# A graph kernel whose start-up norms go by quarters for six tiles instead of four

## The reference

```
mask = adj > 0
head = mask / max(sqrt(sum(mask * mask, rows)), 1e-12)
inc  = adj + head
y    = x + (inc @ x) / sum(inc, rows)
out  = (y - mean(y)) / sqrt(var(y) + 1e-5)        # over the 256 columns
```

## Time and profile before

| | us |
|---|---|
| median of 3 runs | 427.29 (424.83 to 427.61) |
| the profiled execution, its own time | 428.19 |
| its span, first to last instruction | 426.4 |
| PE busy | 396.4 |
| DVE busy | 370.9 |
| POOL busy | 344.2 |
| ACT busy | 343.3 |

### The profile page before, as it was taken

How to read it: one execution, slowest core, us unless ns; L and a number is a source line. 1 busy time by engine, 2 the same in 40 slices (tenths; PEclk the granted TensorE clock), 3 DMA queues, 4 the chain that set the end, 5 groups by cost and what they waited for, 6 DMA issues and landing times.

```text
span 426.4 us, 8925 instructions
## 1 busy us (share of the span) xinstructions
PE 396.4 (93%) x2174; PEld 349.5 (82%) x2174; DVE 370.9 (87%) x750; ACT 343.3 (81%) x450; POOL 344.2 (81%) x273
## 2 busy tenths in 40 slices
PE   1299987989999999999999999999999999999995
PEld 0277866868888888888888888888888888888884
DVE  0986776899999999999999999999999999999942
ACT  4874968989998888888989889898988988886300
POOL 3110386799999999999999999999999999999960
PEclk9999998999999999999999999999999999999999
DMA  8999986666766666666666666776666676670010
GB/s 231 258 233 244 261 220 182 173 190 200 215 188 197 194 203 216 213 196 192 200 184 200 186 200 202 221 212 190 200 186 199 186 199 194 206 221 25 26 38 12
DMA packets 38220, 79.86 MB, mean 187 GB/s; under 512 B 9536, under 2 KB 21824, under 8 KB 38208
## 3 DMA queue, kind: packets, MB, share of 16 engines
q1 hardware_dynamic: 37824, 78.68, 64.8%
q10 hardware_dynamic: 384, 1.05, 0.9%
HBM read 75.50 MB, written 4.19 MB: 187 GB/s over the span
## 4 chain that ended last, share of the span: by engine, by line
PE 70%; issue 3%; POOL 2%; DVE 2%; ACT 0%; POOLq 0%; DVEq 0%
PE edge L699 35%; PE edge L708 18%; PE edge L655 15%; POOL inc_split L380 2%; DVE inc L465 1%; PE sums L650 1%; DVE incT L481 1%; POOL inc_split L385 0%; ACT scaled L237 0%; POOLq L45 0%; POOL rstd L364 0%; DVE rows L533 0%; DVE rows L508 0%; DVE rows L512 0%; DVE stats L516 0%
## 5 line engine op out<-in xcount | busy, mean ns | idle before, releaser
L380 POOL TENSOR_TENSOR inc_split<-incT,inc_split 128x832 fp32r<-128x832 f32 x120 | 236.9, 1985 | 8.9 <-DVE incT L481 6.1
L699 PE MATMUL edge<-x_split,inc_split 128*128 128x512 f32 (+1 forms) x810 | 195.4, 392 | 0.0
L226 ACT ACTIVATE sign_out<-raw,sign_bias 128x1024 bf16<-128x1024 f32 x128 | 146.3, 1143 | 32.0 <-DMA raw<-in_adj_dram 30.5
L699 PEld LDWEIGHTS edge<-x_split,inc_split 128*128 128x128 f32 x810 | 145.9, 188 | 26.7
L465 DVE SCALAR_TENSOR_TENSOR inc<-raw,scaled 128x1024 f32<-128x1024 f32 x128 | 153.5, 1199 | 4.1 <-ACT scaled L237 4.1
L481 DVE STREAM_TRANSPOSE incT<-inc 128x1024 f32<-128x1024 f32 x128 | 155.8, 1227 | 0.2
L237 ACT ACTIVATE scaled<-raw,norm 128x1024 f32<-128x1024 f32 x128 | 141.7, 1107 | 13.2 <-POOL norm L390 6.6
L708 PEld LDWEIGHTS edge<-x_split,inc_split 128*128 128x128 f32 x780 | 99.1, 194 | 2.3
L708 PE MATMUL edge<-x_split,inc_split 128*128 128x256 f32 x780 | 100.0, 286 | 0.0
L655 PE MATMUL edge<-x_native,incT 128*128 128x256 f32 x384 | 92.2, 389 | 1.1 <-DVE count L447 0.7
L655 PEld LDWEIGHTS edge<-x_native,incT 128*128 128x128 f32 x384 | 71.9, 194 | 10.1 <-DVE incT L481 0.8
(11 more groups left out here) (35 smaller groups left out, 119.5 us busy)
## 6 DMA issues: line engine op xcount, KB each, us to landing
raw<-in_adj_dram SPq DMA_DIRECT2D x504, 128.0 KB, 2.6
rows<-in_x_dram SPq DMA_DIRECT2D x32, 128.0 KB, 2.1
out_dram<-rows SPq DMA_DIRECT2D x32, 128.0 KB, 1.7
x_stage<-in_x_dram SPq DMA_DIRECT2D x8, 224.0 KB, 10.3
x_stage<-in_x_dram SPq DMA_DIRECT2D x8, 192.0 KB, 9.8
raw<-in_adj_dram ACTq DMA_DIRECT2D x8, 128.0 KB, 5.4
x_native<-in_x_dram SPq DMA_DIRECT2D x4, 192.0 KB, 7.3
```

Of the source, the lines that this page charges most:

```text
L226: nc.scalar.activation(sign_out[:, :], raw[:, s, q, :], ACT.Sign, scale=SIGN_SCALE, bias=sign_bias[:, 0:1], accum_out=part_sums[:, s, 1, q ...
L380: nc.gpsimd.tensor_tensor(lo_of(s, q), incT[:, s, 0:SPLIT, q, :], hi_of(s, q).bitcast(fp32), ALU.subtract).then_inc(lo_by_pool, 1)
L699: last = nc.tensor.matmul(edge[s][:, c0:c1], inc_split[s][:, 0, b, :, :].rearrange("p q j -> p (q j)"), x_split[:, b, :, :].rearrange("p h ...
```

## The change

- `EARLY` goes from 4 to 6, and tiles 2 and 3 get their degree sum by a product of its own (`sum_degree`) instead of the joint one. PE, DVE, ACT and POOL each get a written list for the tiles up to 5; the lists of the last tiles are written out too, in the order that they had.
- x is loaded so that a run in memory holds two rows (2 KB, before 1 KB). To match, the transpose reads `inc` with a step of two elements: chunk 2b+l holds the columns 64b+2j+l. `X_AT` goes from 0, 7, 14, 20 to 0, 6, 14, 20.
- `sign_out` becomes int8 in two slots, so that a sign waits for the one before the last. Its bias is given as a constant, not as a tile.
- y is built in place; `y_main` goes, and `y_first` waits for the normalisation of tile t-2.
- SP loads the residual of tile 1 behind the adj rows of tile 2, and stores tile t-5 behind tile t's loads (before t-4).
- In the loop the joint sum goes from hi chunk 3 to hi chunk 6.

```diff
-        sign_out = sb("sign_out", [P, COLS], bf16)
+        sign_out = sb("sign_out", [P, 2, COLS], mybir.dt.int8)
...
-    x_v = x.rearrange("(g b j) d -> g j b d", g=G, j=SQ)
+    x_v = x.rearrange("(g b j l) d -> g j b (l d)", g=G, j=SQ, l=2)
...
-        X_AT = [0, 7, 14, 20, SPLIT]
+        X_AT = [0, 6, 14, 20, SPLIT]
-        EARLY = 4
+        EARLY = 6
...
 SP:
+            load_x(0)
+            load_x(1)
+            load_x(2)
+            load_x(3)
+            load_residual(0, 0, False)
+            for k in range(G):
+                load_quarter(2, 0, k, True)
+            load_residual(1, 1, False)
+            for k in range(G):
+                load_quarter(3, 1, k, True)
+            for t in range(4, 6):
+                for k in range(G):
+                    load_quarter(t, t % 2, k, True)
+                if t == 5:
+                    store(0, 0)
+                load_residual(t - 2, t % 2, True)
...
-                    store(t - 4, s)
+                    store(t - 5, 1 - s)
...
 ACT:
-                    act.wait_ge(signs_ready, G * t + q)
+                    act.wait_ge(signs_ready, G * t + q - 1)
...
             sign_early(0, 0)
             sign_early(0, 1)
             scale_early(0, 0)
+            scale_early(0, 1)
             sign_early(0, 2)
-            scale_early(0, 1)
             sign_early(0, 3)
+            sign_early(1, 0)
             scale_early(0, 2)
+            sign_early(1, 1)
             scale_early(0, 3)
-            sign_early(1, 0)
-            sign_early(1, 1)
+            sign_early(1, 2)
...
 DVE:
-                nc.vector.transpose(incT[:, s, :, q, :],
-                                    inc[:, q, :].rearrange("p (b j) -> p b j", j=SQ)).then_inc(incT_ready, 1)
+                nc.vector.transpose(incT[:, s, :, q, :].rearrange("p (b l) j -> p b l j", l=2),
+                                    inc[:, q, :].rearrange("p (b j l) -> p b l j", j=SQ, l=2)).then_inc(incT_ready, 1)
...
+                dve.wait_ge(result_ready, t - 1)
+                after(t, 2)
+                step(nc.vector.scalar_tensor_tensor(y[:, s, :], edge[s][:, D:2 * D], rdeg[:, :], xres[:, s, :],
+                                                    ALU.mult, ALU.add))
...
             count_early(0, 0)
+            inc_quarter(0, 0, 0, reuse=False, reuse_deg=False)
             count_early(0, 1)
-            inc_quarter(0, 0, 0, False, False)
+            transpose_quarter(0, 0, 0, slot_split=False, reuse_slot=False)
             count_early(0, 2)
...
+            inc_quarter(0, 0, 2, reuse=False, reuse_deg=False)
+            inc_quarter(0, 0, 3, reuse=False, reuse_deg=False)
             count_early(1, 0)
             count_early(1, 1)
             count_early(1, 2)
+            transpose_quarter(0, 0, 2, slot_split=False, reuse_slot=False)
+            transpose_quarter(0, 0, 3, slot_split=False, reuse_slot=False)
...
 PE:
-            native_tile(0, 0, {1: lambda: sum_early(1, 2), 6: lambda: sum_early(1, 3)}).then_inc(edge_ready, 1)
-            native_tile(1, 1, {2: lambda: sum_degree(0, 0), 5: lambda: sum_early(2, 0), 9: lambda: sum_early(2, 1),
-                               15: lambda: sum_early(2, 2), 22: lambda: sum_early(2, 3),
-                               28: lambda: sum_early(3, 0)}).then_inc(edge_ready, 1)
-            tile(2, 0, {("native", 0): lambda: sum_degree(1, 1), ("native", 1): lambda: sum_early(3, 1),
-                        ("native", 4): lambda: sum_early(3, 2), ("hi", 6): lambda: sum_early(3, 3),
-                        ("lo", 8): lambda: sum_quadrants(2, 0, early=True)}, first=True)
-            tile(3, 1, {("hi", 18): lambda: sum_quadrants(3, 1, early=True)})
+            sum_early(1, 2)
+            unsplit_chunks(0, 0, 0, B, {4: lambda: sum_early(1, 3), 18: lambda: sum_degree(0, 0)})
+            unsplit_chunks(1, 1, 0, B, {3: lambda: sum_early(2, 0), 8: lambda: sum_early(2, 1),
+                                        14: lambda: sum_early(2, 2), 17: lambda: sum_early(2, 3),
+                                        22: lambda: sum_degree(1, 1), 25: lambda: sum_early(3, 0),
+                                        31: lambda: sum_early(3, 1)})
+            tile(2, 0, {("native", 1): lambda: sum_early(3, 2), ("hi", 11): lambda: sum_early(3, 3),
+                        ("hi", 18): lambda: sum_early(4, 0), ("lo", 1): lambda: sum_degree(2, 0)}, first=True)
+            tile(3, 1, {("native", 0): lambda: sum_early(4, 1), ("native", 4): lambda: sum_early(4, 2),
+                        ("hi", 6): lambda: sum_early(4, 3), ("hi", 14): lambda: sum_early(5, 0),
+                        ("lo", 7): lambda: sum_degree(3, 1)})
+            tile(4, 0, {("native", 0): lambda: sum_early(5, 1), ("native", 2): lambda: sum_early(5, 2),
+                        ("hi", 3): lambda: sum_early(5, 3), ("hi", 14): lambda: sum_quadrants(4, 0, early=True)})
+            tile(5, 1, {("hi", 9): lambda: sum_quadrants(5, 1, early=True)})
+            SUMS_AT = ("hi", 6)
```

More of the change, by code:

```diff
@@ L427, in _ @@
+            norm_early(4, 3)
             low_quarter(3, 1, 3)
-            with pool.Fori(2, PAIRS - 1) as u:
-                tile(2 * u, 0)
-                tile(2 * u + 1, 1)
-            tile(TILES - 2, 0)
-            tile(TILES - 1, 1, more=False)
-            for s in range(2):
-                rstd_of(TILES - 2 + s, s)
+            low_quarter(4, 0, 0)
+            norm_early(5, 0)
+            rstd_of(2, 0)
+            round_quarter(4, 0, 1)
+            round_quarter(4, 0, 2)
+            norm_early(5, 1)
@@ L611, in _ @@
-            tile(TILES - 2, 0, PAIRS - 1)
-            tile(TILES - 1, 1, PAIRS - 1, more=False)
-            normalise(TILES - 3, 1, PAIRS - 2, True)
-            for s in range(2):
-                for _ in residual(TILES - 2 + s, s, PAIRS - 1):
-                    pass
-                normalise(TILES - 2 + s, s, PAIRS - 1, True)
+            transpose_quarter(1, 1, 0, slot_split=False, reuse_slot=False)
+            inc_quarter(1, 1, 2, reuse_deg=False)
+            inc_quarter(1, 1, 3, reuse_deg=False)
@@ new lines, in _ @@
+            count_early(4, 3)
+            inc_quarter(4, 0, 2)
+            y_second(2, 0)
+            statistics(2, 0)
+            count_early(5, 0)
+            transpose_quarter(4, 0, 2)
+            inc_quarter(4, 0, 3)
+            mean_variance(2, 0)
+            variance_eps(2, 0)
+            transpose_quarter(4, 0, 3)
+            degree(3, 1)
+            inverse_degree(3, 1)
+            normalise(2, 0, 1)
+            count_early(5, 1)
+            inc_quarter(5, 1, 0)
+            y_first(3, 1, 1)
@@ new lines, in _ @@
+            variance_eps(26, 0)
+            transpose_quarter(28, 0, 3)
+            inc_quarter(29, 1, 0)
+            degree(27, 1)
+            normalise(26, 0, 13)
+            inc_quarter(29, 1, 1)
+            inverse_degree(27, 1)
+            transpose_quarter(29, 1, 0)
+            y_first(27, 1, 13)
+            inc_quarter(29, 1, 2)
+            y_second(27, 1)
+            count_of(30, 0)
+            transpose_quarter(29, 1, 1)
+            statistics(27, 1)
+            inc_quarter(29, 1, 3)
@@ new lines, in _ @@
+            transpose_quarter(31, 1, 1)
+            statistics(29, 1)
+            inc_quarter(31, 1, 3)
+            mean_variance(29, 1)
+            transpose_quarter(31, 1, 2)
+            variance_eps(29, 1)
+            transpose_quarter(31, 1, 3)
+            degree(30, 0)
+            normalise(29, 1, 14)
+            inverse_degree(30, 0)
+            y_first(30, 0, 15)
+            y_second(30, 0)
+            statistics(30, 0)
+            mean_variance(30, 0)
+            variance_eps(30, 0)
@@ L619, in _ @@
+            degree(31, 1)
+            normalise(30, 0, 15)
+            inverse_degree(31, 1)
+            y_first(31, 1, 15)
+            y_second(31, 1)
+            statistics(31, 1)
+            mean_variance(31, 1)
+            variance_eps(31, 1)
+            normalise(31, 1, 15)
         @block.tensor
```

613 lines of the change are left out of this document (410 added, 203 removed).

## The result

The changed kernel takes 422.51 us (422.11 to 423.53, 7 runs); beside it the kernel before took 427.61. The ratio is 0.9883 with a 95% interval of 0.9849 to 0.9917, so 5.1 us or 1.2% less. The forecast was 8.5 us. The profiled execution took 423.53 (before 428.19). Now and then an execution takes over 1.5% longer than the fastest of the same kernel; such executions are left out of all comparisons here.

The account below looks back on a forecast made before the run. PE was taken as the bound, idle only in start-up. Tile 4 ending at 92.0 instead of 100.72 was to gain 8.5 us, later tiles and tail unchanged: 427.29 - 8.5 = 418.8; forecast 416.5 to 421.5 (64%), range 415.5 to 423.5.

Parts of the forecast that it names:

- the walk: Start-up worked out in order from single durations: tile 0 begins at 25.2, tile 1 ends 54.7, tile 4 ends 92.0 us.
- rival A: Start-up: one new PE wait of 2 to 2.5 us with half clock behind it; gain 4 to 4.5, 423.0 us; 18%.
- When PE can start tile 0: Start-up: with the new engine orders PE begins tile 0 at 25.2 us instead of 21.13.
- Six native chunks take 2.59 us, 0.432 each, so 64 chunks take 27.7: Tiles 0 and 1 on PE: their 64 chunks priced at 0.432 us each, 27.7 us in all.
- Tiles 2 to 4: Start-up on PE: waits of 2.52 and 1.31 us go; three tiles take 37.3 us, ending at 92.0.
- the ten extra sums: Tiles 2 to 4: ten more small sums in PE's list, 0.17 us each, 1.7 in all.
- The nine sums of tiles 0 and 1: Tiles 0 and 1: nine small sums on PE, taken at 0.2 us each, 1.8 in all.
- The 2.52 us go, and with them the clock's fall, 1.7: Tile 2: PE's wait before the joint sum goes, 2.52 us, and the work lost to the lower clock, 1.7.
- x sooner by 1.2 us: Loading x in 2 KB runs: 251 GB/s instead of 234, so x ends 1.2 us sooner.
- The full tiles: The loop after start-up: 27 tiles keep their period of 11.87 us.
- The strided transpose: DVE transposes reading every second element: taken at 1.23 us each, the same as contiguous ones.
- rival C: DVE: the strided read slows transposes; 434 us at 1.5 us each, 533 at the far bound; 6%.

Follow-up runs that it names:

- the dummies: Changed kernel with six unused fp32 products of 256 columns on PE between tile 1's sums, ahead of tile 0: 420.88 us, ratio 0.9831; second run 420.96, 0.9860.
- the added wait: Changed kernel with a PE wait for tile 3's last transpose at lo chunk 2 of tile 2: 426.52 us, ratio 0.9971; without it 422.00, 0.9877.

## Why the prediction was right, and where its size was off

**Right in the walk, lucky in the range.** The waits went where the prediction said, but the gain is 5.1 and not 8.5. The time is inside the stated range only because that range had been widened for rival A, a new wait of 2 to 2.5 us with the clock at half behind it (423.0). No such wait came. The time came near that rival's figure for another reason, the slow first chunks, which stand in no rival. That is luck.

**When PE can start tile 0: right.** 25.2 worked out, 24.82 measured. Of the 0.4, about half is quarter (1,0)'s data, there at 16.34 in place of 16.58; the rest fits signs that take 0.1 less.

**"Six native chunks take 2.59 us, 0.432 each, so 64 chunks take 27.7": this step failed**, by 2.9 us, and it is most of what is missing. The price was taken from a full tile, where PE is busy without a gap. Behind 17 us in which PE did nothing but small sums with gaps, it runs the first chunks at half pace. The trace of the kernel before shows it, too, in a line that I passed over as part of the stretch in which PE waits for x:

```profile
22.45 4.52 PE L655 MATMUL edge<-x_native,incT 128*128 128x256 f32 x10
26.80 0.28 PE L629 MATMUL sums<-part_sums,quad_sum 128*128 128x1 f32 x2
```

Ten records, five chunks, take 4.35 us up to the next sum, 0.87 each, though x_native and incT were there: the first of them ran at 21.13. It cost nothing that shows there, since PE still had to wait for the last piece of x at 37.19. The change moved PE's start behind the point where x covers it, and so uncovered the slow stretch. The granted clock in the records does not tell: the window of PE from 24 to 31 us of the changed kernel (busy, count, clock, DMA share, GB/s) says 1.00, while each chunk takes twice its time. That is the pace of the 1.2 GHz level; that the clock was at that level is inferred from the pace.

```profile
24.00:31.00 7.00, 6.18 (x16) 1.00 1.07 237
```

The Trainium skill, page "TensorE: Matmul & The Clock Gate", section "Part 1: The HAM clock gate", gives the lower rate as the idle state and warns that the trace's clock events have been seen to be unreliable. Both fit this case: 0.9 us a chunk behind the quiet stretch, and 1.00 in the clock column beside it. The prediction looked at clock only where the records showed a fall.

**Tiles 2 to 4: all waits gone, right.** 37.3 us worked out, 37.95 measured. Three times 11.868 is 35.6. If the rest is all the ten extra sums, they cost 2.35, 0.235 each and not 0.17. That is 0.65. The nine sums of tiles 0 and 1 come to 0.23 each, worked out in the same way.

**The reason for the 8.5 was half right.** "The 2.52 us go, and with them the clock's fall, 1.7" treats the two as PE's loss. Taken away alone they gave 0.5 us by the medians (0.8 by the ratio, its interval reaching from 0 to 1.6). Other engines set the pace of that stretch: PE then waited for POOL's round, and with that moved, at the next joint sum. That the joint norm of tile 4 holds them is the likeliest reading, argued and not shown by itself. The prediction's list of waits also left out 0.88 us ahead of the sum of (3,3) at 62.19 and 0.35 us ahead of tile 4. Its walk came out near the truth all the same, because it priced the new lists from end to end and not the waits removed. In the changed kernel the sentence would be true: there a wait costs its length, and by the mean clocks the fall as well in about half of the runs.

**x sooner by 1.2 us: not shown, and without effect.** 240 GB/s, not 251, in the range of what 1 KB runs reach (234 and 245). With tile 0 slow at its start, x had cover in any case; with the dummies ahead it has almost none, and there the run's length was not tested. My reading of 234 against 261 as the price of short runs doesn't hold. The Trainium skill, page "DMA: Bandwidth & Descriptors", section "Specifications", by which 512 B is enough, fits what the runs show here: no gain from 1 KB to 2 KB.

**The full tiles: 11.887 in place of 11.868**, 0.5 us in 27 tiles, not foreseen. With the joint sum at hi 3 again the even period is 11.873, but the first loop tile loses it there. The rest is open.

**The strided transpose: right**, 1225 ns against 1226; rival C falls. The Trainium skill, page "SBUF — State Buffer", section "Door 1: The DMA port swizzle", has two halves here; the trace agrees with the one by which two accesses per 16-byte line go at full rate.

Together: 8.5 - 2.9 (slow chunks) + 0.4 (start) - 0.25 (sums in tiles 0 and 1) - 0.65 - 0.5 (full tiles) = 4.6, and the profiled executions differ by 4.66. The 0.2 allowed for a wait in tile 5 did not come; it is about what separates the two readings of tile 5's start before, 100.72 and 100.56.

Rival A's prices were right in size (a wait of 2.3 costs 2.6, and 1.3 more in about half of the runs), but no such wait came.

## What to carry to other kernels

Price the first products behind a quiet stretch at half pace, whatever the granted clock says: look for a chunk that takes twice its usual time, and ask what covers it. Then fill the quiet stretch with products nobody needs, if the engine has nothing else to do; here six of them are worth about 2 us. Where a forecast's number comes true by a path that none of its theories names, count it as a miss. And before a wait is counted as a gain, look at who sets the pace: in a stretch that others set, a removed wait only moves to the next sum.

## What the hardware showed that was not expected

- The half-speed stretch lasts for four chunks in some traces of the changed kernel and its variants (the changed kernel beside the added wait, the sum at hi 3) and six in others (its first trace, and the one beside the dummies), 3.6 to 5.7 us. By these figures it spreads the time by up to 1 us.
- In the traces, waits of 2.52 us and 2.45 us were followed by a fall of the granted clock (0.57 from 71 to 75 us, 0.65 from 78 to 82 us), one of 2.32 us was not, and one of 4.03 us was followed by 6 us at half.
- ACT's sign with its bias as a constant takes 1042 ns, with the bias read from SBUF 1134. The Trainium skill, page "ScalarE: Activation LUTs", gives about 93 ns for each operand of that kind (section "What ACT_TABLE_LOAD costs"); the trace agrees. The prediction had not counted this edit. Beyond the 0.2 us at tile 0's start no effect on the time is seen.
